# Router scores as a reciprocal of 1 + exp(-x) in an attention and mixture-of-experts block

## The reference

```
x = x + layernorm(attention(layernorm(x)))          # 16 heads of 16, rotary, causal softmax
x = x + layernorm(ffn(layernorm(x)))                # ffn includes its own residual
```

```
logits = xf @ gate_w.T
scores = jax.nn.sigmoid(logits)
sfc = scores + gate_bias                            # decides which experts are taken
...                                                 # groups by the sum of their two best, then the best 4
topk_w = scores[taken] / (sum + 1e-20) * 2.5
y = sum over taken experts of topk_w * expert(xf)  + shared expert(xf)
```

## Time and profile before

| | us |
|---|---|
| three runs | 975.33, 972.92, 973.52 (median 973.52) |
| profiled execution | 975.9 |
| its span, first to last instruction | 974.1 |
| busy: PE, DVE, ACT, POOL | 819.3, 645.0, 453.3, 422.6 |
| granted TensorE clock, mean | 0.899 |

### The profile page before, as it was taken

One profiled execution on the slowest core, in us unless ns is written; L12 is line 12 of the kernel. 1 busy time (PEld: TensorE's weight loads), 2 busy tenths in 40 slices (PEclk: granted clock), 3 DMA queues, 4 the chain that ended last, 5 costly groups with the idle time before them and its releaser, 6 DMA issues.

```text
span 974.1 us, 20032 instructions
## 1 busy us (share of the span) xinstructions
PE 819.3 (84%) x6324; PEld 599.3 (62%) x6324; DVE 645.0 (66%) x1882; ACT 453.3 (47%) x731; POOL 422.6 (43%) x408
## 2 busy tenths in 40 slices
PE   3549887998998997998978978889998999988855
PEld 2426455564664764674744646778886888767722
DVE  5686848689688688789578574653653333977706
ACT  2204535644654554655553547445454555434400
POOL 3132204117527327327304316277577755655521
PEclk9759979898997798998995789899999999989978
DMA  4586843434536435436485403554566657988682
GB/s 174 131 193 159 248 105 99 120 89 141 169 90 175 135 88 173 147 91 188 135 306 179 129 15 106 158 180 136 174 202 214 211 173 268 346 280 311 242 352 96
DMA packets 89173, 168.69 MB, mean 173 GB/s; under 512 B 14704, under 2 KB 56688, under 8 KB 88816
## 3 DMA queue, kind: packets, MB, share of 16 engines
q1 hardware_dynamic: 75248, 128.85, 45.0%
q0 software_dynamic: 13824, 38.55, 10.5%
HBM read 90.15 MB, written 76.68 MB: 171 GB/s over the span
## 4 chain that ended last, share of the span: by engine, by line
PE 44%; DVE 22%; DMA 9%; SPq 8%; ACT 7%; issue 6%; POOL 3%; DVEq 0%; ACTq 0%; POOLq 0%
PE ring L1561 8%; DVE nmax L842 5%; PE ring L1332 5%; PE ring L1334 4%; PE ring L1333 4%; PE ring L1416 4%; PE ring L1582 3%; PE ring L1382 3%; DMA xg<-sorted_rows 3%; PE ring L1346 3%; ACT prob L1262 2%; PE ring L1547 2%; PE ring L1461 2%; DVE nmax L838 2%; PE ring L1401 2%
## 5 line engine op out<-in xcount | busy, mean ns | idle before, releaser
L744 POOL DMA_INDIRECT expert_rows<-ys,dest x160 | 158.9, 993 | 92.3 <-ACT ys L1211 42.1
L842 DVE TENSOR_REDUCE nmax<-ring 128x2 f32<-128x768 f32 (+1 forms) x192 | 158.4, 864 | 40.7 <-PE ring L1389 39.9
L736 POOL DMA_INDIRECT sorted_rows<-xr,idx_all x128 | 126.5, 988 | 108.9 <-DVE xr L1004 75.5
L1262 ACT ACTIVATE prob<-ring 128x1024 f32<-128x1024 f32 x128 | 128.0, 1021 | 96.6 <-PE ring L1407 96.4
L1561 PE MATMUL ring<-we,xh 128*128 x640 | 158.2, 392 | 0.0
L1561 PEld LDWEIGHTS ring<-we,xh 128*128 128x128 f32 x640 | 120.0, 197 | 14.1
L1067 DVE SCALAR_TENSOR_TENSOR sl<-sl,got,ring 128x128 f32<-128x128 f32 x160 | 48.4, 344 | 100.9 <-ACT sl L1314 100.7
L1382 PE MATMUL ring<-k_st,q_st 48*128 48x384 f32 (+3 forms) x512 | 82.5, 382 | 26.7 <-ACT prob L1262 8.7
L1416 PE MATMUL ring<-prob,v_sb 128*32 128x256 f32 (+3 forms) x1024 | 101.2, 493 | 2.0 <-ACT prob L1262 1.9
L714 POOL TENSOR_TENSOR rot<-rot 128x512 f32<-128x512 f32 x14 | 17.9, 1277 | 158.0 <-DVE rot L818 158.0
L1401 PE MATMUL ring<-maskt_b,halves_b 64*128 64x128 bf16 (+2 forms) x640 | 53.1, 248 | 38.3 <-DMA q_st<-mrow 23.3
(11 more groups left out here) (205 smaller groups left out, 1710.0 us busy)
## 6 DMA issues: line engine op xcount, KB each, us to landing
xg<-sorted_rows SPq DMA_DIRECT2D x160, 134.0 KB, 2.8
parts<-part SPq DMA_DIRECT2D x32, 512.0 KB
ykt<-expert_rows SPq DMA_DIRECT2D x14, 1024.0 KB, 9.6
k_st<-parts SPq DMA_DIRECT2D x64, 128.0 KB, 3.8
q_st<-parts SPq DMA_DIRECT2D x64, 128.0 KB, 3.5
we<-w_exp SPq DMA_DIRECT2D x1, 6144.0 KB, 20.4
sorted_rows<-zeros SPq DMA_DIRECT2D x2, 2144.0 KB, 8.9
sorted_rows<-zeros SPq DMA_DIRECT2D x32, 134.0 KB
```

Source lines behind the costliest of these rows:

```text
L736: pool.indirect_dma_start(out=xs[group_of(s)], out_offset=bass.IndirectOffsetOnAxis(ap=idx_all[:, s, t, k:k + 1], axis=0), in_=xr[:, s % 2 ...
L744: pool.indirect_dma_start(out=yk, out_offset=bass.IndirectOffsetOnAxis(ap=dest[:, j % 8, b:b + 1], axis=0), in_=ys[:, j % NYS, b, :], in_o ...
L842: dve.tensor_reduce(nmax[:, Q % 2, :, pp, qb], slot[:, :, col:col + (qb + 1) * P], AX.X, ALU.max, negate=True).then_inc(s_max, 1)
L1262: act_e.activation(prob[:, u % 2, 2 * half:2 * half + 2, 0:width], slot[:, :, 0:width], ACT.Exp, scale=SCALE).then_inc(s_exp, 1)
```

## The change

The scores are computed in three instructions on two engines. ScalarE takes exp(-x) of the logits instead of the Sigmoid, in a step of its own (`SG`) at plan time 29.45, with VectorE's sum of the logits left in `LG` at 29.1. VectorE adds 1.0 and takes the reciprocal, in place, as the first two steps of part 0. The parts of the routing get new times (29.7 + 0.275 i). The norm statistics move from -19.05 to -18.7, behind the logits' sum of the sequence four before, and the normalised rows from -18.05 to -17.9. All these times are shifted by the same 0.5 later on.

```diff
-BEFORE = [("LX", -25), ("LN", -19.05), ("LNR", -18.05), ("XT", -16), ...
+BEFORE = [("LX", -25), ("LN", -18.7), ("LNR", -17.9), ("XT", -16), ...
-         ("GU", 0, 28), ("GU", 1, 28.01), ("GA", 0, 28.5), ("GA", 1, 28.9), ("LGA", 28.75), ("LG", 29.1)]
-AFTER += [("RT", i, 29.5 + 0.29 * i) for i in range(12)]
+         ("GU", 0, 28), ("GU", 1, 28.01), ("GA", 0, 28.5), ("GA", 1, 28.9), ("LGA", 28.75), ("LG", 29.1), ("SG", 29.45)]
+AFTER += [("RT", i, 29.7 + 0.275 * i) for i in range(12)]
...
-ROUTE_STEPS = 30
+ROUTE_STEPS = 32
...
                 dve.wait_ge(s_score, s + 1)
+                step(dve.tensor_scalar(r_sc[:, :], r_sc[:, :], 1.0, None, ALU.add))
+                step(dve.reciprocal(r_sc[:, :], r_sc[:, :]))
                 step(dve.tensor_tensor(r_sf[:, :], r_sc[:, :], kc[:, K_BIAS:K_BIAS + NT * E], ALU.add))
...
-                elif kind == "LG":
+                elif kind == "SG":
                     act_e.wait_ge(s_sumlg, n + 1)
                     if n:
                         act_e.wait_ge(s_route, ROUTE_STEPS * n)
-                    act_e.activation(r_sc[:, :], r_lg[:, :], ACT.Sigmoid).then_inc(s_score, 1)
+                    act_e.activation(r_sc[:, :], r_lg[:, :], ACT.Exp, scale=-1.0).then_inc(s_score, 1)
```

More of the change, by code:

```diff
@@ L94 @@
 ST_TIME = [0.0, 1.0, 1.2, 2.0, 2.2]
-BEFORE = [("LX", -25), ("LN", -19.05), ("LNR", -18.05), ("XT", -16), ("QK", 0, -14.6), ("SPL", 0, -13.6), ("SPS", 0, -12.9),
+BEFORE = [("LX", -25), ("LN", -18.7), ("LNR", -17.9), ("XT", -16), ("QK", 0, -14.6), ("SPL", 0, -13.6), ("SPS", 0, -12.9),
           ("QK", 1, -12.8), ("SPL", 1, -10.9), ("SPS", 1, -10.2), ("V", -5)]
 AFTER = [("X1L", 18), ("AT", 21.6), ("OP", 22.5), ("LNA", 23.7), ("LNB", 24.7), ("LNS", 25.25), ("LNC", 26), ("HT", 27),
-         ("GU", 0, 28), ("GU", 1, 28.01), ("GA", 0, 28.5), ("GA", 1, 28.9), ("LGA", 28.75), ("LG", 29.1)]
-AFTER += [("RT", i, 29.5 + 0.29 * i) for i in range(12)]
+         ("GU", 0, 28), ("GU", 1, 28.01), ("GA", 0, 28.5), ("GA", 1, 28.9), ("LGA", 28.75), ("LG", 29.1), ("SG", 29.45)]
+AFTER += [("RT", i, 29.7 + 0.275 * i) for i in range(12)]
 AFTER += [("SD", 30.5), ("Z", 30.501), ("CNT", 32.2), ("DP", 34.3)]
@@ L454, in block_kernel @@
         s_sumlg = sem("logit_sums")
-        s_score = sem("router_scores")
+        s_score = sem("router_exponentials")
         s_route = sem("router_steps")
```

## The result

The changed kernel takes **958.29 us** (median of 4 runs, 957.05 to 959.86) against 973.22 us (4 runs, 971.76 to 975.33): ratio 0.9857 [0.982, 0.9894], 14.9 us sooner where 8.2 were forecast. The time lies just inside the range (958.0 to 971.5) and outside the likeliest case's own (963 to 968.5); the nearest case was the rival in which the clock comes back as well (961). The profiled execution took 957.2 us, the two profiles differ by 18.7 us in span. Of the kernel before, a second profile was taken later (span 970.1), of the kernel after too (957.9); that pair differs by 12.2 us.

A forecast was written before the change was run, and what follows sets the result against it. ScalarE's table loads ahead of the probability exponentials held up TensorE, with VectorE nearly as late. 2.4 + 1.2 + 2.3 + 0.8 = 6.7 us plus a 1.5 us clock term gave 8.2: 973.5 to 965.3 us, range 958 to 971.5.

The forecast's parts named there:

- the likeliest case: Whole kernel: 8.2 us sooner, 965.3 us, chance 0.54; its own range with the spread of runs 963 to 968.5.
- the rival in which the clock comes back as well: TensorE's clock also recovers in sequences 2 and 5 before the shared down product: 4.2 us more, 961 us, chance 0.22.
- VectorE's sum: Sequences 0, 1 and 3, logits' sum to Z: minus 1.99, 0.85 and 0.52, plus 1.84 and 0.71, 0.81 us sooner.
- The wait for Z: TensorE ahead of the next score product in sequences 0, 1 and 3: grows from 0.3 to some 0.4 to 1.8 us.
- The 0.52: Routing part 3 moves behind Z on VectorE: costs 0.52 us later, hidden in sequence 0, charged in 5 and 6.
- The reciprocal: VectorE's new step over 64 columns: priced at 0.45 us, 0.48 with the gap; trace slope 0.53, add's cost 0.20.
- sequence 5: TensorE's 1.10 us wait for the exponential goes, less 0.52 for part 3, plus a 0.24 wait: gain 0.8 us.
- the clock term: Sequence 4: without the 2.32 us wait the clock holds, 1.5 us less; nothing added in 2 and 5.
- VectorE did not take it all: Rival: in sequences 0 to 3 VectorE's steps cost 0.8 us more, only 4 and 5 give: 970.4 us, chance 0.13.
- The loads did not stay: Rival: loads still surround the new exponential, seven sequences pay 0.71 us: 978.5 us, chance 0.03.
- the slower case: New idle time ahead of the score product behind Z costs clock, 4 us per fall, three falls: 979 us, chance 0.08.
- the prediction's own sign: Falls of the clock to 0.50 in sequences that have none now would make the prediction wrong.

The follow-up runs named there:

- experiment 3: Changed kernel plus an unused one-column Sigmoid right behind the router's exponential, table loads back on the path: 972.34 us, ratio 1.0016 to the kernel before.
- experiment 4: Changed kernel plus the same unused Sigmoid at plan time 30.2, behind the two probability exponentials where ScalarE is idle: 959.69 us, ratio 0.9884 to the kernel before.
- experiment 2: Changed kernel's plan times with Sigmoid kept, no add and no reciprocal: 974.53 us, ratio 1.0021 to the kernel before.
- the function alone: Also experiment 1: exponential, add and reciprocal put in the kernel before, all its plan times kept: 967.84 us, ratio 0.9972 to the kernel before.
- experiment 7: Changed kernel with norm statistics and normalised rows back at their old times (-19.05, -18.05): 959.0 us, ratio 0.9871 to the kernel before.
- experiment 9: Changed kernel with scores finished on ScalarE (Tanh, then Copy with scale and bias), VectorE's add and reciprocal gone: 959.9 us, ratio 0.989 to the kernel before.
- experiment 11: Changed kernel with scores finished on ScalarE and statistics at their old times: 962.11 us, ratio 0.991 to the kernel before.

## Why the prediction was right, and where it failed

**Right: the mechanism and VectorE's sum.** The loads on the path were the cost (experiments 3 and 4), and in sequences 0, 1 and 3 of the first pair the gain is 0.84 to 0.89 us where 0.81 was worked out. The wait for Z stepped in at 1.77 to 1.83 us, the upper end of what was forecast. Sequences 6 and 7 give nothing, as forecast, but for 6 that was luck. There VectorE's waits up to r_m fall by 1.77 us, and the two steps take 1.86 with their gaps, 1.06 of it the add's delay beside a_lo, which the forecast did not have. The 0.52 that it set against the gain for part 3 was no cost: part 3 and Z both stand ahead of r_m in either order.

**The add** cost 0.18 us with the gap kept, as priced, but only because of its place; that GpSimd could hold it up was not among my costs. The row that I priced it from (0.196 us, cw) has no GpSimd instruction beside it. The trace of the kernel before had the warning elsewhere, in sequences 0 to 3: another add of this kind, a quarter as wide, beside GpSimd's `part`, takes 1.27 us, and 0.16 where it is undisturbed.
```profile
221.22 1.27 DVE L989 TENSOR_SCALAR xr<-kc 128x16 f32<-128x16 f32 x1
```
```profile
219.93 2.54 POOL L721 TENSOR_TENSOR part<-rot,part 128x512 fp32r<-128x512 f32 x2 [1.46 <-ACT part L1211]
```

**The reciprocal** takes 553 ns; I took 450, the slope of the earlier trace rows gave 0.53. The Trainium skill's iterated divide ("VectorE: DVE Perf Modes", "First, the fixed hardware budget") led to an estimate of 0.65: nearer than mine from the other side, and the trace's slope was better than both. Between 4 columns and 64, both in SBUF, the slope is (553 - 178) / 60 = 6.25 ns a column. The reciprocal cost the sum 0.1 us more in each of four sequences.

**Failed: sequence 5**, forecast 0.8, measured 4.82 and 3.43. The step was "In 5 the 1.10 goes, but from Z on VectorE works through to r_m": I took TensorE's one wait for the ceiling, and charged part 3 with 0.52, which is no cost here either. The row count there waits for r_m, so what sets the stretch is all that VectorE waits for between the logits' sum and r_m. Its rows with idle time in the kernel before, sequence 5:
```profile
546.83 0.23 DVE L925 TENSOR_TENSOR r_sf<-r_sc,kc 128x64 f32<-128x64 f32 x1 [2.03 <-ACT r_sc L1290]
...
550.28 1.23 DVE L842 TENSOR_REDUCE nmax<-ring 128x2 f32<-128x1024 f32 x1 [1.22 <-PE ring L1389]
...
553.91 0.69 DVE L1194 TENSOR_TENSOR z<-ring,xr 128x512 f32<-128x512 f32 x1 [0.76 <-PE ring L1334]
556.08 0.69 DVE L1194 TENSOR_TENSOR z<-ring,xr 128x512 f32<-128x512 f32 x1 [1.48 <-PE ring L1334]
...
561.77 0.07 DVE L949 MEMSET r_top<- 128x16 f32 x1 [0.53 <-DVE r_top L944]
```
With the 0.24 of the earlier trace rows these are 6.26 us. After the change one is left:
```profile
531.47 1.23 DVE L842 TENSOR_REDUCE nmax<-ring 128x2 f32<-128x1024 f32 x1 [0.67 <-PE ring L1391]
```
6.26 - 0.67 - 0.80 (the two new steps with their gaps) = 4.79; measured 4.82. In the second profile of before the same waits are 2.03, 0.83, 1.26, 0.24 and 0.53, 4.89 in all: 3.42, measured 3.43. The two waits for Z are the shared down product at the half clock, so part of this is the clock; the rest, 2.03 for the Sigmoid above all, was in the rows and not in my sum. In sequence 4 the same sum (2.03 + 0.84 + 1.28 + 0.24 + 1.92 + 0.18 = 6.49 before; 0.67 + 0.80 + 0.93 after) gives 4.09; I had come to 3.8 by another way, TensorE's wait and the clock.

**Mis-sized: the clock term**, 1.5 us, in sequence 4 alone. The fall behind the wait does go with the wait: some 8 us into the stretch, behind a wait of 2.3 to 2.4 us, the clock falls in sequences 1, 3 and 5 of both experiments that keep loads on the path (2 and 3), as in the second profile of before, and in no profile without them. In the profile that I read it stood in 4, with long falls in 2 and 5; sequence 1 had the 2.32 us wait there and no fall behind it, the one of eleven such waits without. In 4 the term was right in that profile (21.87 us with the fall behind the wait, 20.37 in the second profile without). Missing were the others: each such fall was worth 1.16 us in 1 and 3, and the 10.2 us in sequence 2 were worth 2.5 (23.48 against 20.96). In the second pair sequence 2 gave 1.09 (1.2 forecast) and 4 gave 2.66 (2.3 without its clock term), but these come near by luck: the forecast took TensorE's waits of 1.23 and 2.32 us, which are 0.79 and 0.77 in that profile. VectorE's sum gives them as in sequence 5: in 2 its waits fall from 4.53 to 0.80 us, less 0.80 for the steps and 1.84 for the statistics, 1.09; in 4 from 5.22 to 1.74, less 0.80, 2.68. So the clock of one profile was not the kernel's clock, and TensorE's wait moved with it. "The clock comes back in 2 and 5 as well" was a rival at 0.22 that I held back because "the fall came before" the wait of that sequence. In sequences 0 to 3 the changed kernel takes the same time with a fall or without.

**The rivals.** VectorE did not take it all: the price of its steps was right. The loads did not stay. The new idle time ahead of the score product behind Z (1.8 us in four places of the first profile of the changed kernel and one of the second) brought no fall in the rest of its stretch, so the slower case fell, while four of the five 2.32 us waits in the two profiles of the kernel before have one behind them. By the prediction's own sign, falls "in sequences that have none now", the second profile would speak against it: sequence 1 has one. The sign was a poor one, since the kernel before has a fall in sequence 1 too in its second profile, and the changed kernel's stretch is no longer for it.

**What stays open.** Why the function alone stands at 967.8 is settled in part: in the profiles it is 7.0 us above the changed kernel, 5.0 of them in the stretches and 2.9 in the one held-up residual add, less small gains elsewhere. Its median lies 3.6 us above its profiled execution, and what those other runs lose no trace shows. Why L884, which starts first, is the one held up stays open too. How much the places of parts 3, 6 and 7 are worth by themselves was not tried. That falls of the clock take back what VectorE gives in experiments 7, 9 and 11 is read from their traces; no run held the clock fixed to prove it.

## What to carry to other kernels

Price a table load by the instruction that waits behind it, not by its busy time: thirteen loads in idle time cost nothing that the time shows, fourteen on the path 13 us. Where an engine's work ends a stretch, sum that engine's waits from the stretch's start to its end; the waits of the engine that it releases are only part of them. And take the clock term from more than one profile, since falls move from one execution to the next, and a stretch that another engine bounds does not feel them as long as TensorE has idle time left in it. Before pricing a small VectorE instruction, look in the trace for others of its kind beside GpSimd's work.

## What the hardware showed that was not expected

- A small VectorE instruction that starts 0.1 us behind a large GpSimd one waits for its end: 1.23 to 1.28 us instead of 0.16 to 0.22, as TENSOR_SCALAR and as TENSOR_TENSOR alike. In sequence 6 of experiments 9 and 11, where the add is gone, r_sf starts 0.37 us behind a_lo and is held up in its place (0.97 and 0.98 us). One over 128x1024 took 4.02 us instead of 1.23 beside two of GpSimd's, though it started first.
- Not every neighbour does this: r_sf (224 to 226 ns) beside GpSimd's power over 128x4, and the norm statistics beside a_lo (408 to 412 ns each, 404 in the median of the others), are not held up. For r_sf, which has two inputs in SBUF, the Trainium skill's rule told under experiment 1 would have a wait to the end of the power; the rows show none, and the measurement decides.
- The same 3.4 us at the half clock cost 1.16 us or nothing, by whether they lie behind TensorE's wait or ahead of it, where the wait shrinks instead (from 2.32 to 0.96 us in the kernel before, for Z from 1.8 to 0.5 after).
